# Order of the short matmuls in a software-pipelined graph network kernel

## The reference

```
h  = relu(layernorm(x))                       # over the 512 features
# layer 0: graph attention, 8 heads of 64 units
feats = h @ W0                                # 128 x 512
dense = leaky_relu(e_self[:, None] + e_neigh[None, :], 0.2) + (-1e10) * (1 - A)
x1 = x + relu(softmax(dense) @ feats + b0)    # per head
# layer 1: hypergraph convolution, twice
h  = relu(layernorm(x1))
prop(v) = Dinv * (H @ (Binv * (H.T @ v)))     # H = (A != 0)
r  = relu(prop(h @ W1.T) + b1)                # 128 x 1024
y  = prop((layernorm(r) * gamma + beta) @ W2.T) + b2
out = x1 + h + y
```

## Time and profile before

| what | value |
|---|---|
| median of 3 runs | 2612.44 us (2610.91 to 2613.1) |
| the profiled execution | 2612.08 us |
| its span, first to last instruction | 2610.3 us |
| mean granted TensorE clock | 0.995 of full |
| TensorE matmul busy | 98% of the span, 15508 instructions |
| weight loads busy (they overlap matmuls) | 86% |
| VectorE, ScalarE, GpSimd busy | 72%, 58%, 56% |
| chain of work that ended last | 96% TensorE |

### The profile page before, as it was taken

How to read it: one execution, slowest core, us unless ns; L and a number is a source line. 1 busy time by engine, 2 the same in 40 slices (tenths; PEclk the granted TensorE clock), 3 DMA queues, 4 the chain that set the end, 5 groups by cost and what they waited for, 6 DMA issues and landing times.

```text
span 2610.3 us, 51365 instructions
## 1 busy us (share of the span) xinstructions
PE 2559.5 (98%) x15508; PEld 2245.7 (86%) x15508; DVE 1880.3 (72%) x4638; ACT 1518.2 (58%) x3593; POOL 1458.9 (56%) x2196
## 2 busy tenths in 40 slices
PE   4999999999999999999999999999999999999998
PEld 3888888888888888888888888888888888888886
DVE  6777777777777777777777777777777777777774
ACT  3565556556555555656655565565565555556553
POOL 5555555555555555555555555555555555555553
PEclk8999999999999999999999999999999999999999
DMA  4111111111111111111111111111111111111110
GB/s 151 52 55 62 58 60 63 58 60 55 66 60 55 63 58 60 62 59 60 55 62 59 60 63 58 60 57 64 60 54 62 58 60 63 58 60 55 65 51 25
DMA packets 85593, 158.70 MB, mean 61 GB/s; under 512 B 16832, under 2 KB 33216, under 8 KB 85568
## 3 DMA queue, kind: packets, MB, share of 16 engines
q1 hardware_dynamic: 85568, 158.39, 18.0%
HBM read 124.26 MB, written 34.08 MB: 61 GB/s over the span
## 4 chain that ended last, share of the span: by engine, by line
PE 96%; DVE 1%; issue 0%; ACT 0%; POOL 0%; POOLq 0%; DVEq 0%
PE p_w1a L793 14%; PE p_w1a L795 14%; PE p_w1a L794 14%; PE p_att L864 8%; PE p_w1b L793 5%; PE p_w1b L794 5%; PE p_w1b L795 5%; PE p_w1b L898 4%; PE p_att L844 4%; PE p_ta L811 4%; PE p_fa L794 2%; PE p_fa L795 2%; PE p_fa L793 2%; PE p_fb L794 2%; PE p_fb L793 2%; PE p_fb L795 2%
## 5 line engine op out<-in xcount | busy, mean ns | idle before, releaser
L359 POOL TENSOR_TENSOR rs<-ve,halfpow 128x1 f32<-128x1 f32 x128 | 115.0, 898 | 550.6 <-DVE ve L745 550.6
L793 PE MATMUL p_w1a<-W_hi,rT_hi 128*128 128x512 f32 x1024 | 414.8, 405 | 0.0
L794 PE MATMUL p_w1a<-W_lo,rT_hi 128*128 128x512 f32 x1024 | 403.7, 394 | 0.0
L795 PE MATMUL p_w1a<-W_hi,rT_lo 128*128 128x512 f32 x1024 | 403.5, 394 | 0.0
L424 ACT ACTIVATE att<-u,shifts 128x128 f32<-128x128 f32 x1024 | 400.3, 391 | 4.7 <-DVE shifts L705 4.7
L425 ACT ACTIVATE att_low<-u,shifts 128x128 f32<-128x128 f32 x1024 | 400.2, 391 | 0.0
L349 POOL TENSOR_TENSOR u<-u,mask 128x1024 f32<-128x1024 f32 x128 | 307.2, 2400 | 29.2 <-POOL mask L346 17.4
L319 POOL TENSOR_TENSOR ve<-mv,eps 128x1 f32<-128x1 f32 x256 | 93.0, 363 | 411.3 <-DVE mv L630 326.1
L477 ACT ACTIVATE rT_hi<-p_tb 128x512 fp32r<-128x512 f32 x128 | 76.7, 599 | 330.0 <-PE p_tb L811 330.0
L760 DVE SCALAR_TENSOR_TENSOR z<-p_w1a,rs,t_bc 128x512 f32<-128x512 f32 x128 | 96.1, 750 | 218.3 <-PE p_w1a L795 218.3
L864 PE MATMUL p_att<-feats,attT 128*128 128x65 f32 x2048 | 242.5, 271 | 2.2 <-ACT attT L467 2.2
(11 more groups left out here) (127 smaller groups left out, 7128.5 us busy)
## 6 DMA issues: line engine op xcount, KB each, us to landing
u<-en_rows SPq DMA_DIRECT2D x128, 512.0 KB, 3.6
x_in<-in_x SPq DMA_DIRECT2D x128, 256.0 KB, 2.6
out<-raw SPq DMA_DIRECT2D x128, 256.0 KB, 2.1
adj_in<-in_adj SPq DMA_DIRECT2D x128, 128.0 KB, 2.4
en_rows<-eT SPq DMA_DIRECT2D x512, 1.0 KB
raw<-in_W1T SPq DMA_DIRECT2D x2, 1024.0 KB, 11.0
raw<-in_W2T SPq DMA_DIRECT2D x2, 1024.0 KB, 9.8
raw<-in_W0T SPq DMA_DIRECT2D x1, 1024.0 KB, 6.5
```

Of the source, the lines that this page charges most:

```text
L359: nc.gpsimd.tensor_tensor(rs1[:, :], ve1[:, :], halfpow[:, :], ALU.pow).then_inc(s_rs1, 1)
L793: mm(dst, hi, w_hi, start=first, stop=False)
L794: mm(dst, hi, w_lo, start=False, stop=False)
L795: return mm(dst, lo, w_hi, start=False, stop=final)
```

## The change

Two blocks of TensorE's turn change their place; nothing is added or removed, and every wait stays with its block. On the other engines nothing changes. Step 3 (y) now runs ahead of step 2 (the transposes of r), so that steps 2 and 4 adjoin: four and eight transposes. Steps 11 and 12 (G and the transposes of xn) now run directly behind step 9 (the propagation of h), ahead of step 10 (nine matmuls of features), so that steps 9, 11 and 12 adjoin, and `hidden` follows features.

```diff
@@ turn, after hidden @@
                     hidden(g, 1, p_w1b)
-
-                    pe.wait_ge(s_r, g.count(per=2) - 1)
-                    if g.plus(3).within(NG):
-                        pe.wait_ge(s_h0_lo, g.plus(3).count())
-                    transposes(p_ta, r[:, 0:HALF], s_rT)
                 g = t.plus(-1)
                 if g.within(NG):
 ...
                     three(p_tb[:, :], G_hi[:, :], G_lo[:, :], z_hi[:, :], z_lo[:, :],
                           True, True).then_inc(s_y, 1)
+                g = t
+                if g.within(NG):
+
+                    pe.wait_ge(s_r, g.count(per=2) - 1)
+                    if g.plus(3).within(NG):
+                        pe.wait_ge(s_h0_lo, g.plus(3).count())
+                    transposes(p_ta, r[:, 0:HALF], s_rT)
                 g = t.plus(1)
@@ turn, after the propagation of h @@
                     last.then_inc(s_hg, 1)
-                g = t.plus(3)
-                if g.within(NG):
-                    features(2, 1)
-                    features(3, 0)
-                    features(3, 1).then_inc(s_feats, 1)
                 g = t.plus(2)
                 if g.within(NG):
 ...
                     transposes(p_ta, xn, s_xnT)
+                g = t.plus(3)
+                if g.within(NG):
+                    features(2, 1)
+                    features(3, 0)
+                    features(3, 1).then_inc(s_feats, 1)
```

## The result

| | before | changed |
|---|---|---|
| median of 6 runs each | 2610.98 us | 2626.98 us (2626.08 to 2627.39) |
| profiled execution, its span | 2612.08, 2610.3 us | 2626.30, 2624.4 us |
| granted TensorE clock | 0.995 | 0.995 |

The ratio of the runs is 1.0059, with a 95% interval of 1.0046 to 1.0072: slower by 16 us. I had forecast 2623.0 us with a range of 2614 to 2629, and slower with a chance of 0.80. (More runs of the kernel before gave 2611.07 and 2611.46 us; the profiled execution that I worked against lies 1 us above its usual time, so the profiles differ by 14.2 us only.)

What follows compares the result with a forecast made beforehand. TensorE's unbroken turns of about 19.8 us were taken to bound the kernel. Against 2612.08 us, - 1.5 + 9.9 + 0.3 + 0.1 + 2.1 = + 10.9 gave 2623.0 us, range 2614 to 2629.

Steps and rivals of the forecast that it cites:

- a wait of step 9 in steady turns: Failure sign: TensorE waiting for h at its propagation in steady turns would make the forecast fail.
- line 864: Sixteen TensorE matmuls that need attT: expected at 1.80 to 1.82 us a steady turn instead of 1.73.
- a period longer: Sign in the chain of waits: the distance from turn to turn should be 0.07 us longer.
- `hidden` of turn 0: Sign in the ramp: it should start about 2 us later, behind later sums.
- What bounds the kernel: A ramp, some 124 turns of about 19.8 us of unbroken TensorE work, and a short drain.
- Part 1: TensorE's joined short groups: no price per group; two joins in 125 turns give 1.5 us of gain.
- Part 2: y ahead of r's transposes makes ScalarE's attT late: 0.08 us in each of 124 turns, 9.9 us.
- Part 3: Features end later, so VectorE's first copy and eT come 0.5 us later; charged 0, far end 0.3 us a turn.
- rival C: Late eT reaches h and step 9 waits: 0.1 to 0.3 us each turn, 2635 to 2660 us; chance 0.07.
- Part 4: Before turn 0, moved features and xn's transposes delay the sums and W2's preparation: 2.1 us charged (0.5 to 4).
- Rival B: Not slower: attT's delay doesn't arise, VectorE's preparation covers the ramp's features; 2610.6 to 2616 us; chance 0.13.
- Rival D: TensorE's clock falls to 0.50 in some turns; about 2740 us with one turn of twenty; chance 0.01.

Runs made afterwards that it cites:

- e4: Against the kernel before: y ahead of r's transposes, and ScalarE's relu of r's upper half ahead of rT_hi; 2612.87 us, ratio 1.0004.
- e2: Against the kernel before: only the second move, G and xn's transposes directly behind the propagation of h, ahead of features; 2620.03 us, ratio 1.0035.
- e6: Against the kernel before: only ScalarE's relu of r's upper half put ahead of rT_hi; 2612.01 us, ratio 1.0002.
- e1: Against the kernel before: only the first move, y ahead of r's transposes; 2625.05 us, ratio 1.0052.
- e5: Against the kernel before: r's transposes and y's matmuls alternate, and ScalarE's relu of r's upper half goes ahead of rT_hi; 2613.66 us, ratio 1.0010.
- e3: Against the changed kernel: ScalarE's relu of r's upper half put ahead of rT_hi, both moves kept; 2620.49 us, ratio 1.0034 to the kernel before.
- e8: Against the kernel before: y first, G alone behind the propagation, ScalarE's relu of r's upper half ahead of rT_hi; 2611.05 us, ratio 0.9996.

## Why the prediction was right

The forecast of +10.9 us against 14.2 in the profiles holds, but in part by luck. The turns cost 15.1 us where I had 8.4, and the ramp gave 0.9 where I had charged 2.1: an overcharge of 3.0 us hides a part of an undercharge of 6.7. One sign by which I said the forecast would fail did also appear, a wait of step 9 in steady turns (15 of the 18 turns counted above lie between 200 and 2500 us). The rows otherwise came as announced, but for line 864 at 1.78 to 1.79 us instead of 1.80 to 1.82, a period longer by 0.122 us instead of 0.07, and `hidden` of turn 0 not later.

**What bounds the kernel.** As said: TensorE's unbroken turns. Every version's median follows its period to within about 3 us, and runs of one kernel scatter by 1 to 6 us.

**Part 1, the joins.** Right in mechanism: nothing per group. By the starts of the loads the two joins of the change give about 10 ns a turn, against the 12 that I had charged; other spacings shift by as much (e4 above).

**Part 2, attT.** Right to 0.01 us at each step (458 at 0.63, attT at 1.64 us; 51 ns from its end to the load). The wait was 0.079 us in three turns of four. The fourth had 0.139: there ScalarE's 458 starts at 0.71 instead of 0.635 us behind r's first transpose. These are the turns in which the loop of four begins anew, and the trace of before had no row with 458 waiting in such a turn. So the term is 94 ns a turn, 11.7 us for my 9.9. (This and the next numbers are from the starts of the weight loads, mean of 111 turns.)

**Part 3, the late eT.** The delay of VectorE's first copy came as worked out, and so did the DMA wait. I had put its arrival at h at 0, with 0.3 us as the far end. It is 8 ns a turn in the change, 1.0 us, since it decides only in turns in which u waits long for its DMA (GpSimd idle 0.60 us ahead of u on average in those turns, 0.32 in the others); e2 showed that alone it would be 41 ns. Taking 0 for the change was a little too low. The price of rival C (0.1 us a turn at least) was too high, its mechanism true.

**Part 4, the ramp.** This is the step that failed: I had charged 2.1 us, and the changed kernel's ramp was 0.9 shorter. The sums did start 2.0 us later (43.99), but the clock rose earlier as well. These are stretches of the ramp for TensorE (busy us, instructions, granted clock), before and then changed:

```profile
44.00:46.00 2.00, 2.00 (x3) 0.50 0.02 2
71.00:77.00 6.00, 5.55 (x14) 0.52 0.23 89
```
```profile
44.00:46.00 2.00, 2.00 (x6) 1.00 0.01 1
71.00:77.00 6.00, 5.54 (x18) 0.70 0.24 89
```

TensorE's timeline of the changed kernel has the sums and r's first transposes of turn 0:

```profile
43.99 7.03 PE L780 MATMUL p_w1a<-raw,gamma_beta 128*2 128x512 f32 x16
...
78.56 0.60 PE L811 MATMUL p_ta<-ident,r 128*128 128x128 f32 x4
```

The sums ran at 1.00 throughout, where they had run at 0.50 up to 46 us. They took 7.0 us instead of the 9.0 of the earlier trace rows, and ended at the same time. `hidden` of turn 0 started at 71.46 us after 71.45, and spent less of itself at the lower level, so that r's transposes came at 78.56 us instead of 79.49. I had said that the clock's phase could "give or take about a microsecond"; it gave one. That the clock rose early is the luck of the execution and needs no change. e6, in which TensorE's order is the kernel before's throughout, had it as well (0.98 between 44 and 46 us), and e1, also with the old ramp, had not:

```profile
39.99 0.77 PE L915 MATMUL p_tb<-beT,inc 128*128 128x129 f32 x2 [6.65 <-POOL beT L369]
...
78.08 0.60 PE L811 MATMUL p_ta<-ident,r 128*128 128x128 f32 x4
```

From G to r's first transposes of turn 0 that is 38.09 us in e6. It was 38.06 in the change and 39.05 in the profile of the kernel before. Among the executions whose clock rose at 43.9 to 44.4 us the mean is 38.24 us without the second move (e4, e5, e6) and 38.43 with it (the change, e2, e3). `hidden` of turn 0 starts 0.7 us later behind G with the move, and less of it runs at the lower level. So the move's own cost in the ramp is some 0.2 us, an estimate from three executions each, and not 2.1.

**What the sum lacked.** The turn is 122 ns longer: 94 from attT, 8 from h, about -10 from the joins and -5 behind the late line 864. The rest, some 35 ns or 4.3 us, lies in the long matmuls: 11 in W2's 24, 21 in `hidden`, 3 in the features ahead of the propagation. Each is spaced under 1 ns wider, on average 233.0 ns in W2 against 232.4 and 233.2 in `hidden` against 232.5. W2's part comes only with the late attT (e1 and the change have it; e2, e3, e4, e8 have not), and most of that in `hidden` with the second move (e2, e3). What sets this spacing stays open. It is more than the gap between the forecast's +10.9 and the profiles' +14.2; the other pieces add up to about -1 (attT +1.8, h +1.0, behind line 864 -0.6, the joins +0.3, the ramp -3.0, the last turns -0.4).

**Rival B** had its half on the ramp nearly right; the other half, that attT's delay doesn't arise, is refuted. (Its upper end was added up wrongly: 2612.1 - 1.5 + 4 is 2614.6, not 2616.) **Rival D** had nothing for it, though a late load now comes in every turn: the granted clock is 1.00 from 80 to 2600 us, and 0.995 over the whole execution as before.

## What to carry to other kernels

Price a matmul by the distance to the next one, in the chain of waits, not by its record: here a record 80 ns longer cost 5 ns at most, and a wait of 80 ns in each turn showed in no idle time. When work moves on the engine that sets the pace, walk the written order of every engine that reads its result, past the reader itself to what stands behind it; the first loss was two instructions behind the reader that the move delayed. And undo each half of such a change by itself, since two waits can share one slack.

## What the runs showed of the hardware

- A short float32 instruction costs 0.11 us in every place tried here, beside its like (0.87 us for eight) or singly between 512-column matmuls (0.11 us each in e5).
- The same 512-column matmuls of `hidden` are spaced 232.5 ns on average in one order (before) and 233.2 in another (the change), at the same granted clock of 1.00.
- At the start of each fourth turn, ScalarE begins an instruction that waits for r's transposes 0.08 us later than in the others (0.71 against 0.635 us behind the first of them, the change).
